# Layer 2 of a four-layer network: its triangular matrix is built with tokens in rows

## The reference, cut to what matters

```
k = x / max(norm(x), 1e-12)              # per token
v = x @ W_write.T
beta = sigmoid(x @ W_beta.T)             # one number per token
v, k_beta = v * beta, k * beta
# per chunk of tokens, L[i, j] = gamma^(i - j) for i >= j:
A0 = tril(-(k_beta @ k.T * L), -1)
A  = inverse(eye - A0)                   # unit lower triangular
v, k_cumdecay = A @ v, A @ (k_beta * decay)
# scan over the chunks, S is 128x128:
attn  = tril(k @ k.T * L)
v_new = v - k_cumdecay @ S
o     = (k * de) @ S + attn @ v_new
S     = total_decay * S + (k * dw).T @ v_new
```

## Time and profile before

| | |
|---|---|
| median of 3 runs | 1970.0 us (1968.33 to 1970.3) |
| the profiled execution | 1975.67 us, its span 1973.6 us |
| PE busy | 1852.1 us (94%) |
| DVE busy | 1316.3 us (67%) |
| POOL busy | 1187.2 us (60%) |
| ACT busy | 1094.6 us (55%) |
| granted PE clock, mean | 0.984 |

### The profile page before, as it was taken

One profiled execution on the slowest core, in us unless ns is written; L12 is line 12 of the kernel. 1 busy time (PEld: TensorE's weight loads), 2 busy tenths in 40 slices (PEclk: granted clock), 3 DMA queues, 4 the chain that ended last, 5 costly groups with the idle time before them and its releaser, 6 DMA issues.

```text
span 1973.6 us, 32281 instructions
## 1 busy us (share of the span) xinstructions
PE 1852.1 (94%) x10357; PEld 1379.6 (70%) x10357; DVE 1316.3 (67%) x4499; ACT 1094.6 (55%) x2686; POOL 1187.2 (60%) x1726
## 2 busy tenths in 40 slices
PE   5999999989898999899999999999999999899997
PEld 3777777767575666567655767777788877787874
DVE  5875465786869768974898485464466654867673
ACT  5244443667575776477646775464345465444345
POOL 5420002677879878886998884260268755544544
PEclk9999999999899999899999999999999999999999
DMA  8000000001000000000000000000000011000001
GB/s 278 18 7 1 1 1 1 1 1 44 1 1 1 1 1 1 1 1 1 1 1 1 5 9 1 1 8 1 1 4 1 2 29 29 3 1 1 2 12 54
DMA packets 26492, 26.00 MB, mean 13 GB/s; under 512 B 3108, under 2 KB 23724, under 8 KB 25940
## 3 DMA queue, kind: packets, MB, share of 16 engines
q1 hardware_dynamic: 26324, 23.95, 3.9%
HBM read 21.80 MB, written 2.15 MB: 12 GB/s over the span
## 4 chain that ended last, share of the span: by engine, by line
PE 68%; POOL 13%; DVE 9%; ACT 5%; issue 5%; DMA 0%; POOLq 0%; SPq 0%; DVEq 0%; ACTq 0%
PE ps L86 62%; POOL arena L103 12%; PE ps L89 5%; ACT arena L97 4%; DVE arena L103 3%; DVE arena L106 1%; DVE arena L141 1%; POOL arena L106 1%; DVE arena L123 1%; DVE arena L109 1%; DVE arena L126 1%; ACT L97 1%; DMA rows<-in_rows 0%; DVE arena L112 0%; DVE arena L129 0%
## 5 line engine op out<-in xcount | busy, mean ns | idle before, releaser
L103 POOL TENSOR_TENSOR arena<-arena 128x128 f32<-128x128 f32 (+6 forms) x716 | 632.7, 895 | 289.6 <-DVE arena L109 127.7
L97 ACT ACTIVATE arena<-ps 128x128 f32<-128x128 f32 (+11 forms) x1072 | 357.1, 367 | 443.7 <-PE ps L86 364.5
L86 PE MATMUL ps<-arena 128*128 128x128 f32 (+4 forms) x3040 | 485.2, 298 | 33.9 <-DVE arena L103 11.1
L86 PEld LDWEIGHTS ps<-arena 128*128 128x128 f32 x3040 | 402.3, 194 | 124.8 <-issue 52.9
L103 DVE TENSOR_TENSOR arena<-ps,arena 128x128 f32<-128x128 f32 (+4 forms) x672 | 293.2, 448 | 166.7 <-PE ps L86 142.1
L86 PE MATMUL ps<-arena,moe 128*128 128x256 f32 (+1 forms) x1312 | 382.3, 431 | 1.6 <-DVE arena L103 1.0
L97 ACT ACTIVATE arena<-arena 128x128 f32<-128x128 f32 (+2 forms) x772 | 299.0, 438 | 79.5 <-POOL arena L103 61.2
L97 ACT ACTIVATE arena<-ps,cols 128x512 f32<-128x512 f32 x324 | 217.9, 689 | 169.4 <-PE ps L86 153.7
L86 PE MATMUL ps<-arena,cst 128*128 128x360 f32 (+1 forms) x768 | 298.8, 502 | 12.6 <-POOL arena L103 7.5
L86 PEld LDWEIGHTS ps<-arena,moe 128*128 128x128 f32 x1312 | 237.9, 192 | 71.9 <-issue 31.4
L89 PE MATMUL ps<-cst,arena 128*128 128x128 f32 (+2 forms) x1360 | 236.2, 278 | 31.3 <-ACT arena L97 15.6
(11 more groups left out here) (110 smaller groups left out, 2183.0 us busy)
## 6 DMA issues: line engine op xcount, KB each, us to landing
rows<-in_rows SPq DMA_DIRECT2D x1, 2253.0 KB, 9.6
moe<-in_L_ffn_w SPq DMA_DIRECT2D x3, 704.0 KB, 9.5
arena<-in_x SPq DMA_DIRECT2D x4, 512.0 KB, 9.0
wf<-in_wf SPq DMA_DIRECT2D x2, 1024.0 KB, 10.4
arena<-in_L_ffn_W SPq DMA_DIRECT2D x8, 256.0 KB, 3.0
out_dram<-arena SPq DMA_DIRECT2D x4, 512.0 KB, 3.3
wmod<-in_wmod SPq DMA_DIRECT2D x4, 384.0 KB, 8.9
arena<-kept SPq DMA_DIRECT2D x8, 192.0 KB, 3.0
```

What stands on the lines that cost most here:

```text
L86: return UNSENT if self.e is None else self.e.matmul(out, lhsT, rhs, start=start, stop=stop)
L97: return self.e.activation(out, in_, func, bias=bias, scale=scale)
L103: return UNSENT if self.e is None else self.e.tensor_tensor(out, a, c, op)
```

## The change

The matrix is made with the row token in the partitions, so that beta is a scalar of the partition, and the copy that the inversion needs comes from its first transpose. A mask `below` (the transpose of `dec2` less the identity, that is the strictly lower decay matrix) is made once.

```diff
 class Delta (l == 2)
-            self.h, self.brow, self.S = self.a, r.take(512), r.take(128)
-            self.gram = r.take(512)
-            self.kb, ... = (self.gram[:, 128 * i:128 * i + 128] for i in range(4))
+            self.h, self.gram, self.S = self.a, r.take(512), r.take(128)
+            self.tri = r.take(512)
+            self.kb, ... = (self.tri[:, 128 * i:128 * i + 128] for i in range(4))
 inv_pe, n == 0
-                    ins = pe.tr(ps[:, col4(i)], m.G4[:, i, 0:128], ident)
+                    ins = pe.tr(ps[:, col4(i)], m.G4[:, i, 0:128] if n or key[0] == "l3" else m.tri[:, col4(i)], ident)
...
+                if n == 0 and key[0] == "l2":
+                    pe.wait_ge(*at("inv_v", b, 0, *key))
 inv_act, ahead of its loop
+            if key[0] == "l2":
+                yield
+                ps = banks.get(b, "inv_f", 0, *key)
+                act.wait_ge(*at("inv_f", b, 0, *key))
+                act.act(m.M4, four(ps[:, :])).then_inc(*act.up(b, "inv_v", b, 0, *key, free=(b, "inv_f", 0, *key)))
 inv_dve
-            for n in range(7):
+            if key[0] == "l2":
+                yield
+                dve.wait_ge(*at("inv_m", b, *key))
+                dve.tt(four(m.Y), four(m.tri), over(neg(0)), ALU.mult).then_inc(*dve.up(b, "inv_y", b, 0, *key))
+            for n in range(1 if key[0] == "l2" else 0, 7):
 l2_pe
+            if b == 0:
+                pe.tr(ps[:, 128:256], dec2[:, 0:128], ident)
...
-                ps = banks.take(pe, b, b, "d2b", g)
-                pe.wait_ge(*at("d2beta", b, g))
-                for i in range(4):
-                    ins = pe.mm(ps[:, col4(i)], m.bt[:, i:i + 1].broadcast_to([128, 128]), ident)
-                ins.then_inc(*pe.up(b, "d2b", b, g))
-                yield
...
-                    ins = pe.mm(ps[:, 0:128], m.vn, m.brow[:, c], start=True, stop=(t == 0))
+                    ins = pe.mm(ps[:, 0:128], m.vn, m.gram[:, c], start=True, stop=(t == 0))
 l2_act
-                ps = banks.get(b, "d2b", g)
-                act.wait_ge(*at("d2b", b, g))
-                act.act(m.brow, ps[:, :]).then_inc(*act.up(b, "d2brow", b, g, free=(b, "d2b", g)))
-                yield
 l2_dve
+            if b == 0:
+                dve.tt(below, ps[:, 128:256], ident, ALU.subtract).then_inc(*dve.up(b, "below"))
...
+                dve.wait_ge(*at("below"))
+                for i in range(4):
+                    dve.stt(m.tri[:, col4(i)], ps[:, col4(i)], m.bt[:, i:i + 1], below, ALU.mult, ALU.mult).then_inc(
+                        *dve.up(b, "d2tri", b, g))
                 dve.tt(four(m.gram), four(ps[:, :]), over(dec2[:, 0:128]), ALU.mult).then_inc(
-                    *dve.up(b, "d2gram", b, g, free=(b, "d2a", g)))
+                    *dve.up(b, "d2am", b, g, free=(b, "d2a", g)))
 l2_pool
-                pool.wait_ge(*at("d2gram", b, g))
-                pool.tt(m.M4, four(m.gram), over(strict), ALU.mult).then_inc(*pool.up(b))
-                pool.wait_ge(*pool.last(b))
-                pool.wait_ge(*at("d2brow", b, g))
-                pool.tt(m.M4, m.M4, four(m.brow), ALU.mult).then_inc(*pool.up(b))
-                pool.wait_ge(*pool.last(b))
-                pool.tt(m.M4, m.M4, over(ident), ALU.subtract).then_inc(
+                pool.wait_ge(*at("d2tri", b, g))
+                pool.tt(four(m.tri), four(m.tri), over(ident), ALU.subtract).then_inc(
                     *pool.up(b, "inv_m", b, "l2", g))
-                pool.cp(m.brow, m.gram).then_inc(*pool.up(b, "d2am", b, g))
```

```diff
-    "pe": ("0123440000000001100110133000221100022210001122133311133200031100122021100012221100022210003311122200"
+    "pe": ("0123440000110011100011003301000111223300033311122222320001113322230001110033301122200012233111000321"
```

More of the change, by code:

```diff
@@ L335, in __init__ @@
         if l == 2:
-            self.h, self.brow, self.S = self.a, r.take(512), r.take(128)
-            self.gram = r.take(512)
-            self.kb, self.kTg, self.akt, self.vn = (self.gram[:, 128 * i:128 * i + 128] for i in range(4))
+            self.h, self.gram, self.S = self.a, r.take(512), r.take(128)
+            self.tri = r.take(512)
+            self.kb, self.kTg, self.akt, self.vn = (self.tri[:, 128 * i:128 * i + 128] for i in range(4))
             self.kd, self.oT = r.take(128), self.kb
@@ new lines @@
+    "act": ("0123400011010011100030011233233234222332240100112221311330001112000220011313302120103132022301201233"
+           "3201321000203030031023102110202013100010110102301222130212312001112210333211313213202110022123023102"
+           "3111331031013321212303023211232100111322211132102100311100013012301011110003010233231022000111013012"
+           "3102001112002220213103100020031111023322212200010211111222032123313012000001112221331130220321322222"
+           "3333032000010022232113332111313111131333211320222312132330331232001222011112002233333010020012131110"
+           "1310033330313220111121223011113000010333133322022120201112210002310101111132103300033031211111222021"
+           "1333323013200002330312022322000320113333011132030222002002310113233303222302000203001121332232231131"
+           "2302133322203221320011101010322333322212300220003133333012300031110312033331330000012021112123102130"
+           "1110000101332232223302100011122012033120120000111110222212333201000301330211131112022232000002302102"
+           "2220200000033332332222230323312220233320011000232222333232003110001220222002322011333011132011130000"
+           "0210333313022322021111131000013333302232220120010322011311203331333012000011101201232222000120201111"
+           "0123222200002010331113313120022210020111200011333313203222133221311120122112002300000102003133332303"
+           "2222232113113313023003212221212213333323030033203313000100220212201133330300220222031111020301112033"
+           "3122000313320220021030333303233222002302220033301033233233332203020002333222113223310120322210033300"
+           "2311020022201101112201310113133133113131313331113331111333223212312322113330113301211330231310022323"
+           "3010220122002012012300120321101233131303123311002200132103210021320120231203220112311012301123303122"
+           "3120032021223300321023130230102301030211001321123313322132331021002130012312311220300232002131100113"
+           "0002233311313113203223113221011303003202332220101310332233111222100133133311203323330222201021230213"
+           "3330313223003000112331100111200321130231123020300010220032022333331001111221331101011332200310213103"
+           "3233003123032001322002123311212111100322311003231123232003323332331122222220330022003301221133111002"
+           "2001111031133112330223110022112333311002222000022322333222233223333"),
@@ L531, in program @@
         mhalf = sb("mhalf", [128, 8])
+        below = sb("below", [128, 128])[:, :]
         gm = sb("gm", [128, 2])
```

155 lines of the change are left out of this document (83 added, 72 removed).

## The result

The changed kernel takes 1946.89 us (1944.79 to 1949.7, 4 runs) where the kernel before took 1970.15 (1968.33 to 1970.84): ratio 0.9884, 95% interval 0.9867 to 0.9902. Forecast was 1961, 9 us faster with a range down to 1949.

What follows compares the result with a forecast made beforehand. PE, busy 94% of the span, was taken as the bound, with POOL a second limit in layer 2. Terms -7.1 + 0.1 - 2 + 0 = -9.0 us took the median from 1970.0 to 1961, range 1949 to 1977.

Steps and rivals of the forecast that it cites:

- PE-bound: PE ends layer 2's attention stage, busy 92% of the stretch; the main forecast, chance 0.44, 1954 to 1966 us.
- the 32 matmuls at -7.1 us on the path: Spreading beta on PE in layer 2: 0.89 us a group, eight groups, removed for -7.1 us.
- No idle time before them: PE has no idle time before the spreading matmuls, so they stand in a full queue, on the path.
- The chain of a group, forecast 2.3 us shorter: From the end of `d2a` to the first `inv_p` in layer 2: 5.9 us before, 3.6 after.
- What that latency is worth ... I take a third of 6.3, -2.: Layer 2's shorter chain saves 0 to 15.0 us of PE idle time; taken as -2, from 6.3 us waiting for POOL.
- Rival B: POOL's chain is worth more: PE's 15.0 idle us go nearly all, or new order saves elsewhere; -20, 1950 us, chance 0.15.
- only 6.3 of the 15 were waits for POOL: Argument against Rival B: of PE's 15.0 idle us in layer 2's stretch, only 6.3 were waits for POOL.
- The new strings at 0, 8 either way: New order of all engines' work, bounded by PE idle time outside layer 2: 0, about 8 us either way.
- Y with two SBUF inputs: DVE's Y reading only SBUF may be blocked by POOL: 0 to 10 us of DVE, taken as hidden, 0.
- DVE's SBUF-only scalings: With POOL's 26 us fewer, these DVE instructions, 440 ns against 347 from PSUM, should run shorter.
- POOL lighter by 26 us: POOL loses two products and a copy, 3.3 us a group, 26 in all; counts only by PE's waits.
- The signs that were to show the forecast right: PE busy near 1845, waits for POOL under 6.3, idle outside layer 2 within 8 of 106, Y not over 1.2 us.

Runs made afterwards that it cites:

- g_old_spread: a_old_order with the 32 matmuls that spread beta put back on PE, in the old order strings: 1973.55 us, 1.0005 of the kernel before.
- c_spread_back: Changed kernel with the 32 spreading matmuls put back on PE, results unread, new order strings: 1948.69 us, 0.9873 of the kernel before.
- b_new_order: Code of the kernel before, run in the changed kernel's order strings with the old spreading and copy steps put in: 1967.71 us, 0.9968 of before.
- d_pool_back: Changed kernel with POOL's two products put back ahead of the subtraction and its copy behind, new strings: 1979.98 us, 1.0029 of before.
- i_jitter1: Changed kernel with order strings before 1200 us sorted anew, random element shifts of up to 1.5 us: 2106.59 us, 1.0681 of before.
- k_y_bank: Changed kernel with each inversion's first Y read from the PSUM bank again and ACT's copy behind it: 1949.37 us, 0.9883 of before.
- a_old_order: Changed code run in the order strings of the kernel before, without the steps that spread beta: 1967.06 us, 0.9957 of before.
- f_pool_load: Changed kernel with the same POOL work as d_pool_back put behind the inversion's first two POOL steps, new strings: 1959.65 us, 0.9936 of before.
- after_again: The changed kernel run and traced once more, no edit: 1948.44 us, 0.9881 of the kernel before.

## Why the prediction was wrong, point by point

- "PE-bound", and the 32 matmuls at -7.1 us on the path: borne out in the old strings, where they are worth 9.4 (g_old_spread); in the new strings, which are those of the change, they are worth nothing that shows (c_spread_back). "No idle time before them" told of the order that was written, not of the work. As this term carried most of the forecast's -9, that the direction came out right was in good part luck.
- The chain of a group, forecast 2.3 us shorter: measured 2.7 (8.2 to 5.5, b_new_order to the changed kernel, same strings). The difference was right, the chains themselves were not: forecast 5.9 and 3.6, measured 9.8 before (8.2 in the new strings) and 5.5. DVE's four products (1.03 to the next start, forecast 1.15), the subtraction and the copy had about their forecast lengths; the waits between the steps had no term.
- **The step that failed: "What that latency is worth ... I take a third of 6.3, -2."** It was bounded by PE's idle 15.0 us and by its 6.3 us of waits for POOL. In the new strings the shorter chain and the lighter POOL are worth 16.5 to 18.7 us (b_new_order against the changed kernel and against c_spread_back, the first with the matmuls' removal in it; each good to some 4 us): far over the 6.3, and by its value over the 15.0. In the old strings they are worth nothing that shows (g_old_spread). PE's waits for POOL hardly fell, from 6.3 us to 6.0; it is the old code in the new strings that shows the latency as waits, 12.7 us. PE's idle time in a stretch of the old profile is what the old strings left: they had put other matmuls where the matrix was late, so the latency stood in the profile as order, not as waits. Part of the cost also comes as busy time at the lower clock, 10 to 16 us of the 33 to 35 between the traces of the changed kernel and d_pool_back. How the 16.5 to 18.7 us divide between the chain's latency and POOL's load is open. Rival B was nearest, and its first half (POOL's chain is worth more) is the one that the runs bear out; "only 6.3 of the 15 were waits for POOL" was the wrong argument against it. B's own way was not seen either: the stretch's 15.0 idle us went to 12.3, not nearly all.
- The new strings at 0, 8 either way: alone they give 6 (b_new_order), inside that band. The band was right only for strings written with care: strings sorted anew with random shifts of up to 1.5 us cost 131 to 157 us. And the sum took code and strings as terms to be added; 8 of the 23 us belong to both together.
- The clock had no term. Over all executions the granted clock was 0.985 to 0.986 in the kernel before, by set, and 0.990 in the changed one (0.982 in d_pool_back, 0.972 in i_jitter1). At a mean of 0.9858 the part of the span lost is 28 us, at 0.9902 it is 19: some 9 of the 23 us are seen as clock. Whether this follows only from fewer idle stretches of PE is not shown by a run of its own; the order of the kernels by clock is nearly that by time.
- Y with two SBUF inputs: 720 ns in the changed kernel, mean of 8, longest 0.96 us, against 685 from PSUM, so 0 was right, and taking it back (k_y_bank) gives nothing. The rule of the Trainium skill (SBUF — State Buffer, "Who interferes with whom") is not contradicted: in a_old_order, where all eight Ys fall together with POOL's work (five in the changed kernel), the mean is 857 ns and the longest 1.4 us. It had no price here that shows. DVE's SBUF-only scalings did run shorter, 372 ns against 393 over the whole span, but they take 370 with POOL's old work in the new strings, so in the new strings the lighter POOL gives nothing there (in the old ones, 381 with it).
- POOL lighter by 26 us: 26.9 measured. Put back where it does not stand ahead of the transposes, this work costs 11 us (f_pool_load), which the prediction had at nothing.
- The signs that were to show the forecast right mostly came: PE's waits for POOL in the stage 6.0 (under 6.3), those for ACT and DVE 5.7 against 6.4, PE's idle time outside the stretch of 1410 to 1600 102.1 (within 8 of 106; 97.9 in after_again), Y under 1.2 us. The time was off all the same: signs read from idle time and waits did not tell a gain of 9 us from one of 23. PE's busy time did differ (1828.6 and 1835.0 against 1845).

## What to carry to other kernels

Where the order of the engines' work is fixed in advance, PE's busy share and its waits show what that order left, not what the work needs: a latency can be hidden as other work put in front, so neither bounds the worth of shortening it. Code and order must be measured as a two by two (each alone, then both): here the shorter chain gave nothing that shows in the old order and some 17 us in the new one, and a small bend of the old order cost more than that. Moving a piece of such a chain from the slower engine to the faster one can still pay, though the chain gets no shorter by it: the subtraction, 1.28 us on POOL and 0.7 on DVE, gave another 5 us.

## What the runs showed of the hardware that was not expected

PE's waits can come with a lower clock, so that they cost more than their length. Against the two traces of the changed kernel, d_pool_back has 18.7 and 22.9 us more idle time of PE and 16.1 and 9.7 us more busy time for the same records; i_jitter1 has 97.5 and 101.7 more idle time with 59.9 and 53.5 more busy time. But idle time alone does not set it. In 1410 to 1600 the granted clock was 0.92 in d_pool_back with PE idle 30.6 us, and 0.99 in f_pool_load with 25.0:

```profile
1410.00:1600.00 190.00, 165.02 (x1271) 147.83 (x1270) 121.86 (x409) 93.70 (x307) 137.41 (x283) 0.99 0.02 6
```

What in the waits makes the difference is not shown. And 32 fp32 matmuls of 128x128, 0.89 us for four back to back, cost 9.4 us in one order and nothing that shows in another.
